# One pipelined fp32 stage in place of three in a two-layer transformer kernel, and another layout for the heads' keys and values

## What is computed

```python
h = layernorm(x) * (1 + ca) + sa
# attention across the 32 heads of one token (D = 16)
q, k, v = ((h @ W.T + b).reshape(B, S, 32, 16) for W, b in ((Wq, bq), (Wk, bk), (Wv, bv)))
scores = einsum('bshd,bsgd->bshg', q, k) * D ** -0.5
scores = where(scores > 0.001, scores, -inf)
attn = softmax(scores)
x = x + ga * (einsum('bshg,bsgd->bshd', attn, v).reshape(B, S, 512) @ Wo.T + bo)
h = layernorm(x) * (1 + cb) + sb
logits = h @ route_w.T                       # 8 experts, the best one kept with its logit
out = einsum('bser,eor->bso', route_weight[..., None] * einsum('bsd,erd->bser', h, A), Bw)
x = x + gb * out
```

## Time and profile before

| | us |
|---|---|
| median of 3 executions (lowest, highest) | 2551.21 (2549.51, 2552.23) |
| the profiled execution | 2552.01 |
| its span, first to last instruction | 2550.4 |
| PE busy | 2029.6 (80%) |
| DVE busy | 1572.9 (62%) |
| POOL busy | 1108.5 (43%) |
| ACT busy | 1029.2 (40%) |

### The profile page before, as it was taken

One profiled execution on the slowest core, in us unless ns is written; L12 is line 12 of the kernel. 1 busy time (PEld: TensorE's weight loads), 2 busy tenths in 40 slices (PEclk: granted clock), 3 DMA queues, 4 the chain that ended last, 5 costly groups with the idle time before them and its releaser, 6 DMA issues. The chain is left out here.

```text
span 2550.4 us, 34479 instructions
## 1 busy us (share of the span) xinstructions
PE 2029.6 (80%) x11904; PEld 1680.7 (66%) x11904; DVE 1572.9 (62%) x3747; ACT 1029.2 (40%) x2380; POOL 1108.5 (43%) x866
## 2 busy tenths in 40 slices
PE   7489999999999942954447999999999996357634
PEld 1378888888888832743335888888888885346434
DVE  1666666666666669244645666666666666852645
ACT  1255555555555522122114555555555553131211
POOL 0454555555554534132325555555554544341322
PEclk9699999999999976965768999999999999678566
DMA  5300100010001001285031100010001001024921
GB/s 228 108 17 26 42 18 26 18 41 26 17 26 42 17 30 54 79 91 125 15 119 34 33 17 26 21 39 25 17 26 42 17 26 38 23 72 90 94 87 42
DMA packets 188903, 123.30 MB, mean 48 GB/s; under 512 B 107172, under 2 KB 151204, under 8 KB 187700
## 3 DMA queue, kind: packets, MB, share of 16 engines
q1 hardware_dynamic: 174356, 101.26, 16.1%
q10 hardware_dynamic: 14368, 19.78, 2.4%
HBM read 100.01 MB, written 21.01 MB: 47 GB/s over the span
## 5 line engine op out<-in xcount | busy, mean ns | idle before, releaser
L965 POOL TENSOR_TENSOR gqa_rot<-gqa_rot,consts 128x512 f32<-128x512 f32 x160 | 209.1, 1307 | 640.8 <-ACT gqa_rot L786 640.7
L802 ACT ACTIVATE gqa_prob<-gqa_prob,gqa_nmax 128x128 f32<-128x128 f32 (+3 forms) x512 | 282.0, 552 | 198.6 <-DVE gqa_nmax L887 198.6
L887 DVE CUSTOM_DVE_ANT_0 gqa_prob<-gqa_pS,consts 128x128 f32<-128x128 f32 (+3 forms) x512 | 220.2, 486 | 73.6 <-PE gqa_pS L686 72.6
L430 PE MATMUL ln_pT<-consts,ln_xn 128*128 128x128 f32 x256 | 59.8, 422 | 253.9 <-DVE ln_xn L409 253.9
L895 DVE TENSOR_TENSOR gqa_ptl<-gqa_pT,gqa_pth 128x384 fp32r<-128x384 f32 (+1 forms) x384 | 218.3, 597 | 31.7 <-ACT gqa_pth L812 27.1
L430 PEld LDWEIGHTS ln_pT<-consts,ln_xn 128*128 128x128 f32 x256 | 51.3, 225 | 262.3 <-DVE ln_xn L409 262.3
L812 ACT CAST gqa_pth<-gqa_pT 128x384 fp32r<-128x384 f32 (+1 forms) x384 | 182.7, 511 | 94.4 <-PE gqa_pT L701 94.3
L968 POOL TENSOR_TENSOR gqa_full<-gqa_full,gqa_rot 128x512 f32<-128x512 f32 x160 | 206.7, 1292 | 12.6
L740 PE MATMUL gqa_pW<-woh,gqa_oh 128*128 128x512 f32 x504 | 202.7, 402 | 9.0 <-DVE first_y L912 9.0
L659 PE MATMUL gqa_pj<-first_hh,wqh 128*128 128x512 f32 x496 | 205.5, 414 | 0.0
L740 PE MATMUL gqa_pW<-woh,gqa_ol 128*128 128x512 f32 x504 | 197.3, 392 | 0.0
(11 more groups left out here) (221 smaller groups left out, 5299.9 us busy)
## 6 DMA issues: line engine op xcount, KB each, us to landing
raw_q<-in_wq SPq DMA_DIRECT2D x16, 1024.0 KB, 5.3
raw_o<-in_wo SPq DMA_DIRECT2D x16, 1024.0 KB, 5.1
mod_wm<-in_wmod SPq DMA_DIRECT2D x8, 1536.0 KB, 19.9
raw_kv<-in_wkv SPq DMA_DIRECT2D x16, 512.0 KB, 6.5
x<-in_x SPq DMA_DIRECT2D x4, 1024.0 KB, 6.4
kp<-qkv_rest SPq DMA_DIRECT2D x16, 256.0 KB, 2.3
qp<-qkv_rest SPq DMA_DIRECT2D x16, 256.0 KB, 2.3
vp<-qkv_rest SPq DMA_DIRECT2D x16, 256.0 KB, 2.3
```

The costliest lines, as they stand in the source:

```text
L802: ins = nc.scalar.activation(p, p, ACT.Exp, scale=-1.0, bias=nmax[r][:, i:i + 1], accum_out=den[r][:, i:i + 1])
L887: nc.vector.tensor_tensor_reduce(prob[r][:, P_OFF[i]:P_OFF[i] + w], pS[s][:, c:c + w], held.mask[:, T - w:T], -1.0, LARGEST, ALU.add, ALU.min,
L965: nc.gpsimd.tensor_tensor(rot[r % 2][:], rot[r % 2][:], held.sinT, ALU.mult).then_inc(sined, 1)
```

## The change

- In the projections V comes first. A V tile is written by DVE into 32 groups of 17 floats (16 values and a 1 that is set once), and stored by 4 DMAs into a DRAM array laid out as quarter, head, token slot, tile, 17. K and Q follow; their arithmetic is as before.
- In head attention `kd` and `bd` have j (or r) ahead of the token slot. The key loads are the same calls on the new layout; a value load reads one run for each partition, ones included. The matmuls read both buffers through a stride. The memsets of the ones fall away.
- The weights of the out-projection and the low-rank matmuls are loaded by SP while head attention runs, after its fourth unit's scores are requested.
- `stage_attention_out`, the norm ahead of the expert stage and `stage_lora` are replaced by one stage, `stage_finish`, all of whose matmuls take unrounded fp32 operands, one product each. It works on the two batch elements in turn. The bias is multiplied by the gate and added to x by POOL. Its SP queue loads, in this order, the attention result of the first element by quarters, the bias, both rows of the first gate, the result of the second element, both rows of the second gate.

The diff, cut to its core (`normalise` and the middle of `choose` are the old lines for four tiles; the two removed stages are printed above):

```diff
-QKV_ORDER = (1, 0, 2)
+QKV_ORDER = (2, 1, 0)
...
+    def load(self, sp):
+        sp.dma_start(self.w[:], self.a["w1o"].rearrange("(k p) n -> p k n", p=P)).then_inc(self.came, 16)
...
+    def load(self, sp):
+        sp.dma_start(self.wA[:, :, 0:NE * R1], self.a["loraAT"].rearrange("(k p) n -> p k n", p=P)).then_inc(self.came, 16)
+        sp.dma_start(self.wA[:, :, NE * R1:], self.a["routeT"].rearrange("(k p) n -> p k n", p=P)).then_inc(self.came, 16)
+        sp.dma_start(self.wB[:], self.a["loraBT"]).then_inc(self.came, 16)
...
+        rest = [st.sb(f"rest{i}", [P, H1 * VW]) for i in range(NB)]
         ps = [st.ps(f"ps{i}", [P, T]) for i in range(8)]
...
-                        dst = a["vp"][b].rearrange("(t r) x -> r t x", r=KT)[m]
-                        sp.dma_start(dst, src[:]).then_inc(stored[n % NB], 16)
+                        for r in range(4):
+                            sp.dma_start(a["vp"][b, r, :, :, m].rearrange("g l x -> l g x"),
+                                         values(n)[r * LO:(r + 1) * LO]).then_inc(stored[n % NB], 16)
                     else:
...
-                        if n - 8 < FIRST_V:
-                            pe.wait_ge(left, n - 7)
+                        if n - 8 < NV:
+                            pe.wait_ge(turned, n - 7)
                         else:
-                            pe.wait_ge(turned, n - 7)
...
+                for n in range(NV, N):
+                    w, b, m = items[n]
...
-                    if n >= NB:
+                    if n >= NV + NB:
...
+                for i in range(NB):
+                    nc.vector.memset(values(i)[:, :, D1:], 1.0).then_inc(ones, 1)
+                dve.wait_ge(ones, NB)
                 for n in range(N):
                     if n >= NB:
-                        dve.wait_ge(stored[n % NB], 16 * (n // NB))
-                    if n < FIRST_V:
-                        dve.wait_ge(left, n + 1)
-                        nc.vector.transpose(rest[n % NB][:], flat[n % NB][:]).then_inc(turned, 1)
+                        dve.wait_ge(stored[n % NB], stored_by[n - NB])
+                    if n < NV:
+                        dve.wait_ge(full, n + 1)
+                        nc.vector.tensor_tensor(values(n)[:, :, 0:D1], ps[n % 8][:].rearrange("p (g x) -> p g x", g=H1),
+                                                vbias[:].rearrange("p (g x) -> p g x", g=H1), ALU.add).then_inc(turned, 1)
                     else:
-                        dve.wait_ge(full, n + 1)
-                        nc.vector.tensor_tensor(rest[n % NB][:], ps[n % 8][:], vbias[:], ALU.add).then_inc(turned, 1)
+                        dve.wait_ge(left, n - NV + 1)
+                        nc.vector.transpose(rest[n % NB][:, 0:T], flat[n % NB][:]).then_inc(turned, 1)
             @block.gpsimd
...
+        kd = [st.sb(f"kd{i}", [P, 4, 4 * LU, H1]) for i in range(NU)]
+        bd = [st.sb(f"bd{i}", [P, 4, 4 * LU, VW]) for i in range(NU)]
         sc = [st.sb(f"sc{i}", [P, TC, H1]) for i in range(NR)]
         prob = [st.sb(f"prob{i}", [P, TC, H1]) for i in range(NR)]
...
             for r in range(4):
-                t0 = (LO * r + l0) * KT
-                src = a["vp"][b, t0:t0 + KT * LU, :].rearrange("t (g x) -> g t x", g=H1)
-                eng.dma_start(bd[u % NU][32 * r:32 * r + 32, :, r, 0:D1], src).then_inc(v_in[u], 16)
+                src = a["vp"][b, r, :, l0:l0 + LU].rearrange("g l j x -> g (l j) x")
+                eng.dma_start(bd[u % NU][32 * r:32 * r + 32, r], src).then_inc(v_in[u], 16)
...
+                            mm = pe.matmul(pS[c % NS][32 * r:32 * r + 32, 4 * l:4 * l + 4, :],
                                            qq[u % NU][0:ROWS, l0 + l, r * H1:(r + 1) * H1],
-                                           kd[u % NU][0:ROWS, 4 * (l0 + l) + r].rearrange("p j g -> p (j g)"), start=True, stop=True)
+                                           kd[u % NU][0:ROWS, :, 4 * (l0 + l) + r, :], start=True, stop=True)
...
+                                           bd[u % NU][:, :, s0 + 4 * l + j, :], start=True, stop=True)
                     mm.then_inc(o_full, 1)
...
+def stage_finish(nc, held, a, out, ws, half):
...
+        ps = [st.ps(f"ps{i}", [P, D]) for i in range(3)]
...
+        users = ([("o", j) for j in range(NT)] + [("a", j) for j in range(TT)] + [("b", j) for j in range(TT)]
+                 + [("a", j) for j in range(TT, NT)] + [("b", j) for j in range(TT, NT)])
+        emptied = {"o": o_gated, "a": a_left, "b": z_gated}
...
+        def wait_bank(pe, kind, j):
+            n = users.index((kind, j))
+            if n >= BANKS:
+                k, i = users[n - BANKS]
+                pe.wait_ge(emptied[k], i + 1)
...
+                pool.wait_ge(bo_in, 16)
+                pool.wait_ge(ga_in, 16 * HB)
+                for b in range(HB):
+                    nc.gpsimd.tensor_tensor(bg[:, b], bo[:], ga[:, b], ALU.mult).then_inc(bias_gated, 1)
                 for j in range(NT):
+                    pool.wait_ge(bias_gated, j // TT + 1)
+                    nc.gpsimd.tensor_tensor(x[:, j, :], x[:, j, :], bg[:, j // TT], ALU.add).then_inc(biased, 1)
+                for j in range(NT):
+                    pool.wait_ge(z_gated, j + 1)
+                    nc.gpsimd.tensor_tensor(x[:, j, :], x[:, j, :], zg[j % 2][:], ALU.add).then_inc(added, 1)
...
+                def project(b):
+                    for j in range(b * TT, (b + 1) * TT):
+                        wait_bank(pe, "o", j)
+                        for k in range(KT):
+                            pe.wait_ge(a_in[b][k], 16)
+                            mm = pe.matmul(bank("o", j)[:], at[:, k, j * P:(j + 1) * P], out.w[:, k, :],
+                                           start=(k == 0), stop=(k == KT - 1))
+                        mm.then_inc(o_full, 1)
...
+                def down(b):
+                    pe.wait_ge(scaled, (b + 1) * KT)
+                    for j in range(b * TT, (b + 1) * TT):
+                        wait_bank(pe, "a", j)
+                        for k in range(KT):
+                            mm = pe.matmul(bank("a", j)[:, 0:NA], hf[:, k, j * P:(j + 1) * P], ws.wA[:, k, :],
+                                           start=(k == 0), stop=(k == KT - 1))
+                        mm.then_inc(a_full, 1)
...
+                def turn_weights(b):
+                    pe.wait_ge(routed, b + 1)
+                    if b:
...
+                def up(b):
+                    pe.wait_ge(w_left, b + 1)
+                    for j in range(b * TT, (b + 1) * TT):
+                        wait_bank(pe, "b", j)
+                        t = slice(j % TT * P, (j % TT + 1) * P)
+                        pe.matmul(bank("b", j)[:], wtT[:, b, t], ws.wB[:], start=True, stop=True).then_inc(b_full, 1)
+                project(0)
+                project(1)
+                turn(0)
+                down(0)
+                turn(1)
+                turn_weights(0)
+                up(0)
+                down(1)
+                turn_weights(1)
+                up(1)
...
+                def features(b):
+                    t = slice(b * T, (b + 1) * T)
                     act.wait_ge(turned, b + 1)
+                    for k in range(KT):
+                        nc.scalar.activation(hf[:, k, t], pT[k][:], ACT.Identity, bias=held.modh[:, 1, 2, k, b:b + 1],
+                                             scale=held.modh[:, 1, 3, k, b:b + 1]).then_inc(scaled, 1)
+                def lowered(b):
+                    for j in range(b * TT, (b + 1) * TT):
+                        act.wait_ge(a_full, j + 1)
+                        nc.scalar.copy(hs[:, j, :], bank("a", j)[:, 0:NA]).then_inc(a_left, 1)
+                def weights_left(b):
+                    act.wait_ge(w_turned, b + 1)
+                    nc.scalar.copy(wtT[:, b], pW[:]).then_inc(w_left, 1)
+                features(0)
+                lowered(0)
+                features(1)
+                weights_left(0)
+                lowered(1)
+                weights_left(1)
...
+                def residual(b):
+                    for j in range(b * TT, (b + 1) * TT):
+                        dve.wait_ge(o_full, j + 1)
+                        nc.vector.tensor_tensor(yg[j % 3][:], bank("o", j)[:], ga[:, b], ALU.mult).then_inc(o_gated, 1)
+                        dve.wait_ge(o_gated, j + 1)
+                        dve.wait_ge(biased, j + 1)
+                        nc.vector.tensor_tensor(x[:, j, :], x[:, j, :], yg[j % 3][:], ALU.add).then_inc(x_new, 1)
+                        dve.wait_ge(x_new, j + 1)
+                        nc.vector.bn_stats(stats[:, j, :], x[:, j, :]).then_inc(stat_done, 1)
+                def normalise(b):
...
+                def choose(b):
+                    s = slice(b * TT, (b + 1) * TT)
+                    wide = [P, TT, NE]
+                    logits = hs[:, s, NE * R1:]
+                    dve.wait_ge(a_left, (b + 1) * TT)
```

(57 more changed lines are left out.)

261 lines of the change are left out of this document (103 added, 158 removed).

## The result

The changed kernel takes 2486.2 us (median of 4 runs, 2480.9 to 2488.7) where the kernel before, on the same chip, takes 2551.7: a ratio of 0.974, 95% interval 0.973 to 0.976. So it is faster by 65 us, half of the 122 that I forecast, and 8 us above the top of my range, 2478. The profiled execution took 2484.1 us, with a span of 2482.4.

A forecast was written before the change was run, and what follows sets the result against it. Bounds: PE in projections, small-packet DMA with low-clock compute beneath in head attention, a chain of waiting stages in the tail. Gains 40 (tail) + 22 (attention) - 1 (projections) = 61 a pass, 122 in all: 2552 to 2430 us; 8-in-10 range 2404 to 2478.

The forecast's parts named there:

- Cost 1 a pass: Projection stage: V stores at 20 ns a piece, 5.1 us a tile, mostly hide behind TensorE; 1 us lost a pass.
- cost 24: Projection stage: at 35 ns a piece the V stores end near 1103 and a pass loses 24 us.
- rival 1: Projection stage: 68-byte stores cost 35 ns like 512-byte ones, up to 24 us more a pass, 2476 in all; 15%.
- Start, pace, the output's wait and the final store: Head attention: first scores after 7.9 us, chunks 2.93 apart, ninth output waits 4.8, final store and barrier 8.0.
- done by 19 us: Merged stage: POOL's added bias gate products and 8 adds, 1.25 us each, finished by 19 us.
- residual(0): Merged stage, first batch: gate product, add and statistics, 2.1 us a tile, ending 20.9 us after the stage's start.
- normalise(0): Merged stage, first batch's norm: 7.8 us from the earlier trace, ending 28.7 us after the stage's start.
- up(1): Merged stage, second batch's low-rank up products: 6.3 us at the low clock, ending 70.4 us after the stage's start.
- Strided operands (3): Head attention: four-piece strided reads halve TensorE's rate, 40 us a pass dearer, 2510 in all; 5%.
- The high clock in the attention's fill (2): TensorE at high clock in attention's fill and both `up` parts: 4 + 6 us a pass more gain, 2410; 10%.
- A stage that doesn't overlap (5): Merged stage stays serial, dearer products eat its gain; about 2510 in all; 1%.
- Slower than before (4): Projection stage: V stores alone make the kernel slower, from 54 ns a packet; 2616 at 70 ns; 2%.

The follow-up runs named there:

- e_p68: Changed kernel with each 68-byte value piece starting at a multiple of 128 bytes in the DRAM scratch: 2459.5 us, timed once.
- e_v80: Changed kernel with each value piece padded to 20 floats, 80 bytes at multiples of 16 bytes: 2445.6 us, timed once.
- a_again: The changed kernel, unaltered, timed once more on another occasion: 2476.1 us, ratio 0.9711 to the kernel before.
- e_gather_mid: Changed kernel with a batch's four value tiles stored together in 272-byte pieces and the weight loads between the two attention-output stores: 2433.4 us, ratio 0.9543.
- e_merge_only: Kernel before with only the merged last stage added, its weights loaded behind the last unit's loads in head attention: 2473.0 us, ratio 0.9698.
- e_v132: Changed kernel with each value piece padded to 33 floats, 132 bytes laid 132 bytes apart: 2506.5 us, timed once.
- e_v128: Changed kernel with each value piece padded to 32 floats, 128 bytes at multiples of 128 bytes: 2444.4 us, ratio 0.9579.

## Why the prediction was wrong, and where it was right

**The step that failed** is the term "Cost 1 a pass" of the projection stage, and in it the price of a V store. I had the place, the mechanism (the ring of four buffers waits for the stores) and the formula; of the price I had two ends, 8 ns for 4-byte writes and 35 for 512-byte ones, and I took 20 "since 68 B is nearer to their size", from reads. The size was the wrong thing to be near to. The pieces of 68 bytes lie 68 bytes apart and cost 33 ns, 8.5 us a tile where I had named anything over 6 as a sign of being wrong; 128 apart they cost my 20 (e_p68), padded to 80 bytes 21 (e_v80), and the stage then does end near 1097, as I forecast. The sum at 35 ns, "cost 24", is what happened: 24.7 and 24.8. It is rival 1, to which I gave 15%. That its number, 2476, is a_again's time is chance: two other terms were off as well, and partly cancel.

By the starts of stages, the two passes lost 49 up to attention where I had 2: 47 more. Attention adds 15 (5 and 10 short of 2 x 22), and the merged stage takes 8 away (88 for 80): 2430 + 47 + 15 - 8 = 2484, the time of the profiled execution.

**Head attention: 17 and 12 where I had 22.** Start, pace, the output's wait and the final store came as forecast. Missing was the place in the queue: the weights' loads went ahead of the fifth unit's keys, and I had them only as bytes (1.3 MB). e_gather_mid shows what that costs: 2442.3 against 2433.4, though from different chips, is 4 to 5 us a pass; within the traces attention is 2.1 shorter in pass one and 3.2 in pass two. The keys of the second to fourth unit wait 2 to 3 us more, which I had at nothing. Pass two gained 5 less than pass one, half because its attention was 2.3 shorter before, half because it is 2.5 longer after: the fifth unit's keys waited 5.15 there and the ninth output 5.46.

**The merged stage: 43 and 45 where I had 40.** S+70.4 against S+72.3, by steps that partly cancel. The first add waited for the gates' loads and for GpSimd's additions of the gated bias, which I had "done by 19 us" without a reader in their way: VectorE's first add comes at S+12.9, a tile takes 2.9 us for my 2.1, since its add takes 1.55 us beside GpSimd, and residual(0) ends at S+23.9 (forecast 20.9). Against it normalise(0) took 5.2 us for the 7.8 I carried over from the earlier trace rows. The links there worked on 4 columns too, but the first three of them (lines 400 to 402) took 0.56, 1.25 and 1.19 us while GpSimd was working, until 1244.05; in the merged stage GpSimd had stopped at 1220.8, ahead of them, and they took 0.17 each. So both sizes came from rows taken with GpSimd in the other state than it had later: the add of the earlier trace rows from a stretch in which it stood still, the norm from one in which it worked. That GpSimd is the cause fits all these rows, but no run changed it alone. And `up(1)` ran at the high clock (granted 1.00), 3.70 us for 6.3 (four products of 1.71 are 6.8, a slip in the sum). e_merge_only gives this gain by itself: 42.

**Rivals.** Strided operands (3): refuted, the groups took 1.93 and 1.13 us as before. The high clock in the attention's fill (2) did not come: 3.64 us for two groups, clock 0.50. A stage that doesn't overlap (5): refuted. Slower than before (4): the price was 33 ns and even the worst layout, 39 ns in e_v132, stays at 2506.5, below the 54 ns from which I had it decide.

## What to carry to other kernels

Lay the small pieces that a DMA writes to HBM a multiple of 16 bytes apart, or fill them up to 128: here 15 unused floats behind the 17 made the kernel 34 to 42 us faster (e_v128 against a_again and the change, by their ratios), and 3 unused floats nearly as much (e_v80, timed once). If a small layout is wanted, gather in SBUF until the piece is several times longer. Loads that are moved ahead belong behind whatever on the same queue is awaited next, and ahead of nothing that is: the same four DMAs made the keys wait 3.3 us in one place, the ninth output 9.2 for 4.8 in another, and in the third the fifth unit's keys did not wait and the output waited 5.2. A duration carried over from another stage should come from rows in which the other engines do what they will do there. And before one argues over the price of a product, one looks who is waiting: half of the products away changed nothing.

## What the runs showed of the hardware

- A write of 68 bytes to HBM costs 20 or 33 ns of an engine by the distance of the pieces (128 or 68 bytes); 132 bytes 132 apart cost 39 ns, 128 bytes 128 apart 14 ns. I had not expected a factor of nearly three between neighbours in size.
- The price of the pieces 68 bytes apart isn't steady: 7.5 to 8.5 us a tile for the same code, while the medians of the kernel before stayed within 0.1% (2549.5 to 2551.7).
- The share of engine time in a view can pass 100% (128.6%): the records of packets overlap there. The elapsed price, 69 us x 16 / 32,038 = 34 ns, is the one that the stage feels, not 44.
- VectorE's add of two SBUF operands takes 1.55 us while GpSimd adds, and 0.69 after it has stopped at 1220.8 (first row below, and 1227.95 above); its product with one operand in PSUM stays at 0.68, and its statistics of one SBUF operand at 0.69. The Trainium skill, "GPSIMD Engine Reference", section "1. Specifications", says that GpSimd shares its SBUF interfaces with VectorE and that instructions with two SBUF inputs contend; this trace agrees.

```profile
1209.62 11.19 POOL L1432 TENSOR_TENSOR x<-x,fin_bg 128x512 f32<-128x512 f32 x8
```

In the kernel before, the links of the norm on 4 columns and GpSimd's last product beside them:

```profile
1241.01 0.56 DVE L400 TENSOR_SCALAR ln_var<-ln_mv 128x4 f32<-128x4 f32 x1
1241.61 1.25 DVE L401 TENSOR_SCALAR ln_step<-ln_var 128x4 int32<-128x4 int32 x1
1242.89 1.19 DVE L402 TENSOR_SCALAR ln_rstd<-ln_step 128x4 int32<-128x4 int32 x1
...
1244.51 0.17 DVE L406 TENSOR_SCALAR ln_step<-ln_step 128x4 f32<-128x4 f32 x1
```

```profile
1242.79 1.26 POOL L300 TENSOR_TENSOR lora_bl<-rawB,lora_bh 128x512 fp32r<-128x512 f32 x1
```
